# The second layer's expert products by high and low parts, with a ring of four experts' weights, in a two-layer graph and expert kernel

## The reference, cut to what matters

```python
def ffn_l1(x, Wg, bg, W1, b1, W2, b2):         # x: 1354 x 256, normed
    probs = softmax(x @ Wg + bg)
    comb = probs * top2_mask(x @ Wg + bg)
    out = zeros_like(x)
    for e in range(8):
        h = gelu(x @ W1[e] + b1[e])            # 256 -> 1024
        y = h @ W2[e] + b2[e]                  # 1024 -> 256
        out = out + comb[:, e:e+1] * y
    return x_residual + out
```

## Time and profile before

| what | value |
|---|---|
| median of 3 runs | 1015.61 us (1013.77 to 1016.34) |
| the profiled execution's own time | 1013.27 us |
| its span, first to last instruction | 1011.5 us |
| mean granted clock of TensorE | 0.896 |
| PE matmul busy | 828.7 us (82%) |
| VectorE / ScalarE / GpSimd busy | 519.4 / 383.4 / 104.4 us |
| bytes moved by DMA | 101.57 MB, mean 100 GB/s |

### The profile page before, as it was taken

The page is one execution under the profiler, slowest core; times in us unless marked ns, Lnnn a source line. Parts: engine busy times, 40 slices in busy tenths (PEclk is TensorE's granted clock), DMA queues, the critical chain, the costliest instruction groups (busy, mean ns, idle before and its releaser), DMA issues.

```text
span 1011.5 us, 12855 instructions
## 1 busy us (share of the span) xinstructions
PE 828.7 (82%) x3873; PEld 576.6 (57%) x3874; DVE 519.4 (51%) x1076; ACT 383.4 (38%) x787; POOL 104.4 (10%) x92
## 2 busy tenths in 40 slices
PE   5968799999999996229999266973549999999993
PEld 4856555555555435129999254862316666666663
DVE  4035587666666738529888236956412222222220
ACT  1004314655556564016666143312003444444441
POOL 2000000000000000260000400000621111111111
PEclk9987859999999998759999677997569999999997
DMA  7498811233230110042542482407231221221212
GB/s 262 166 265 310 214 32 38 58 72 78 70 78 23 33 28 9 10 150 106 198 164 83 138 336 86 143 20 313 77 109 28 32 32 32 32 33 32 35 27 65
DMA packets 53654, 101.57 MB, mean 100 GB/s; under 512 B 17614, under 2 KB 46054, under 8 KB 51920
## 3 DMA queue, kind: packets, MB, share of 16 engines
q1 hardware_dynamic: 47328, 92.20, 28.6%
q0 software_dynamic: 6288, 8.89, 4.8%
HBM read 70.80 MB, written 25.35 MB: 95 GB/s over the span
## 4 chain that ended last, share of the span: by engine, by line
PE 73%; DVE 10%; issue 5%; DMA 4%; POOL 3%; ACT 2%; SPq 1%; POOLq 0%; ACTq 0%; DVEq 0%
PE ps L1165 11%; PE ps L932 10%; PE ps L1147 10%; PE ps L912 6%; PE ps L863 5%; PE ps L924 5%; PE ps L1096 4%; PE ps L1017 4%; PE ps L1019 3%; PE ps L1018 3%; PE ps L1156 3%; DVE mx L1304 2%; PE ps L851 2%; PE ps L1111 1%; POOL xs_d L652 1%
## 5 line engine op out<-in xcount | busy, mean ns | idle before, releaser
L1304 DVE TENSOR_REDUCE mx<-ps 128x1 f32<-128x452 f32 x264 | 148.0, 620 | 68.6 <-PE ps L912 67.3
L718 ACT ACTIVATE expo<-ps 128x452 f32<-128x452 f32 x264 | 124.3, 552 | 110.7 <-PE ps L924 109.7
L932 PE MATMUL ps<-expo,v_st 128*64 128x452 f32 (+1 forms) x576 | 116.2, 525 | 0.0
L912 PE MATMUL ps<-k_st,q_st 96*128 96x452 f32 x264 | 111.3, 451 | 4.8 <-DMA k_st<-k_hi_d 4.6
L1165 PE MATMUL ps<-w_l,h 128*128 x464 | 109.3, 389 | 6.6 <-ACT h L834 4.1
L834 ACT ACT_TABLE_LOAD x29 | 37.2, 1283 | 191.1 <-PE ps L1156 191.1
L1147 PE MATMUL ps<-w_l,x1t_t 128*128 x232 | 107.6, 608 | 1.6 <-DVE x1t_t L1603 1.6
L1165 PEld LDWEIGHTS ps<-w_l,h 128*128 128x128 f32 x464 | 86.9, 192 | 24.7 <-issue 13.7
L924 PE MATMUL ps<-q_st,k_st 98*128 98x452 f32 x264 | 96.9, 388 | 2.5 <-ACT expo L718 2.0
L1615 DVE COPY h1pre<-ps 128x1024 f32<-128x1024 f32 x29 | 35.5, 1224 | 109.0 <-PE ps L1147 109.0
L912 PEld LDWEIGHTS ps<-k_st,q_st 96*128 96x128 f32 x264 | 54.4, 207 | 51.7 <-DVE mx L1304 30.8
(11 more groups left out here) (235 smaller groups left out, 1258.2 us busy)
## 6 DMA issues: line engine op xcount, KB each, us to landing
w_l<-w_l SPq DMA_DIRECT2D x8, 2053.0 KB, 8.3
w_l<-w_l SPq DMA_DIRECT2D x2, 8208.0 KB, 23.6
adj<-adj_t SPq DMA_DIRECT2D x22, 704.0 KB, 4.1
xs_d<-zeros SPq DMA_DIRECT2D x1, 3842.5 KB, 26.4
x1t<-xs_d SPq DMA_DIRECT2D x29, 132.5 KB, 2.1
q_st<-q_hi_d SPq DMA_DIRECT2D x16, 176.0 KB, 3.1
k_st<-k_hi_d SPq DMA_DIRECT2D x16, 176.0 KB, 4.1
xs_d<-zeros SPq DMA_DIRECT2D x1, 2176.0 KB, 10.2
```

The costliest lines, as they stand in the source:

```text
L718: act.activation(expo[g % 8][:, :], ps[:, 3 + g % 3, 0:QC], ACT.Exp, scale=SCALE).then_inc(s_exp, 1)
L912: pe.matmul(ps[:, i % 3, 0:KC], q_st[h % 3][0:3 * DK, (n // KB) * P:(n // KB + 1) * P], k_st[h % 3][0:3 * DK, (n % KB) * KC:(n % KB + 1) * ...
L932: return pe.matmul(ps[at:at + 2 * DK, 6 + g // T % 2, lo:hi], v_st[h % 2][:, kt, :], expo[g % 8][:, lo:hi], start=kt < 2, stop=kt == T - 1 ...
L1304: dve.tensor_reduce(mx4[:, n // KB, n % KB:n % KB + 1], ps[:, i % 3, 0:KC], AX_X, ALU.max).then_inc(s_mx, 1)
```

## The change

The second layer's products are now sums of three one-pass products of high and low parts, as in the first layer.

- **The split.** GpSimd, after L621, takes the weights of all eight experts in 32 parts of 128 x 1024: it loads a part, copies it rounded (`part_hi`), writes it to a scratch tensor in memory, subtracts, and writes the low part. The two part buffers lie where the router's buffers lie, so VectorE waits for all low writes ahead of `choose(0)`.
- **The ring.** Four experts' split weights lie on chip (4 x 8192 columns). SP loads slots 2 and 3 and slots 0 and 1 where it loaded the two halves before, and each of experts 4 to 7 into the slot of expert e - 4 once that one's tiles are done; PE waits for the loads that its tile needs.
- **The tile.** Rows and h1 are split into high and low parts by new operations on VectorE and ScalarE. In the down product the high and low weights of a block lie side by side, so one product of 512 columns makes both, and VectorE adds the two halves. PE's order becomes h1_turn(t + 1), xs1_in(t + 3), up1(t + 2), down1(t); the h1 parts have two buffers. Row loads move from SP's queue to GpSimd's. The biases get a buffer and a load of their own.

The diff, cut to its core:

```diff
+RING = 4
+SPLIT = 1024
+SLOTCOLS = 2 * B1AT
-        w_l1 = place("w_l1", [E, W1COLS])
+        w_ring = place("w_ring", [RING, SLOTCOLS], F32R)
+        part_hi = place("part_hi", [SPLIT], F32R)
+        cursor[0] = offsets["lgt"]
+        part = [place(f"part{i}", [SPLIT]) for i in range(2)]
+        cursor[0] = offsets["lgt"]
+        part_lo = [place(f"part_lo{i}", [SPLIT], F32R) for i in range(2)]
+        w_split_d = scratch("w_split_d", [P, E, SLOTCOLS])
+        PARTS1 = E * B1AT // SPLIT
...
         @block.sync
...
+            sp.wait_ge(s_hi_out, 16 * PARTS1)
+            for k in range(2):
+                sp.wait_ge(s_lo_out[k], 16 * (PARTS1 // 2))
+            sp.dma_start(w_ring.bitcast(F32)[:, RING // 2:RING, :], w_split_d[:, RING // 2:RING, :]).then_inc(s_w1, 16)
...
+            sp.dma_start(w_ring.bitcast(F32)[:, 0:RING // 2, :], w_split_d[:, 0:RING // 2, :]).then_inc(s_w1, 16)
-            sp.wait_ge(s_scat1, 2 * 16 * T)
-            sp.dma_start(x1t[:, :], xs1_d[0:P, :]).then_inc(s_x1l, 16)
...
+            for e in range(RING, E):
+                due = sp.value_load(ends_due[0:1, e - RING:e - RING + 1], min_val=PRIMED + 1, max_val=PRIMED + TILES1)
+                sp.wait_ge(s_y1_ps, due)
+                sp.dma_start(w_ring.bitcast(F32)[:, e - RING, :], w_split_d[:, e, :]).then_inc(s_ring, 16)
+                sp.wait_ge(s_ring, PRIMED + 16 * (e - RING + 1))
...
         @block.gpsimd
...
+            def load_part(n):
+                e, c = divmod(n, B1AT // SPLIT)
+                if n >= 2:
+                    pool.wait_ge(s_lo_out[n % 2], 16 * (n // 2))
+                pool.dma_start(part[n % 2][:, :], a["w_l1"][:, e, c * SPLIT:(c + 1) * SPLIT]).then_inc(s_part[n % 2], 16)
+
+            def split_rows(n, low):
+
+                e, c = divmod(n, B1AT // SPLIT)
+                if c < DT * F // SPLIT:
+                    return w_split_d[:, e, LO1 * low + c * SPLIT:LO1 * low + (c + 1) * SPLIT]
+                at = AT2 + 2 * (c * SPLIT - DT * F)
+                return w_split_d[:, e, at:at + 2 * SPLIT].rearrange("p (f b n) -> p f b n", b=2, n=D)[:, :, low, :]
...
+            load_part(0)
+            for n in range(PARTS1):
+                k = n % 2
+                if n + 1 < PARTS1:
+                    load_part(n + 1)
+                pool.wait_ge(s_part[k], 16 * (n // 2 + 1))
+                if n:
+                    pool.wait_ge(s_hi_out, 16 * n)
+                pool.tensor_copy(part_hi[:, :], part[k][:, :]).then_inc(s_part_split, 1)
+                pool.wait_ge(s_part_split, 2 * n + 1)
+                pool.dma_start(split_rows(n, 0), shaped(n, part_hi.bitcast(F32))).then_inc(s_hi_out, 16)
+                pool.tensor_tensor(part_lo[k][:, :], part[k][:, :], part_hi.bitcast(F32)[:, :],
+                                   ALU.subtract).then_inc(s_part_split, 1)
+                pool.wait_ge(s_part_split, 2 * n + 2)
+                pool.dma_start(split_rows(n, 1), shaped(n, part_lo[k].bitcast(F32))).then_inc(s_lo_out[k], 16)
+            pool.wait_ge(s_hi_out, 16 * PARTS1)
...
+            def load_rows1(t):
+                if t:
+                    pool.wait_ge(s_x1_ps, t)
+                    pool.wait_ge(s_share, t)
+                pool.dma_start(x1t[:, :], xs1_d[t * P:(t + 1) * P, :]).then_inc(s_x1l, 16)
+
+            pool.wait_ge(s_scat1, 2 * 16 * T)
+            for t in range(4):
+                load_rows1(t)
             pool.wait_ge(s_sum0, 16)
             for t in range(TILES1):
+                if t + 4 < TILES1:
+                    load_rows1(t + 4)
                 pool.wait_ge(s_y1, PRIMED + t + 1)
...
         @block.scalar
...
-                last.then_inc(s_h1, 1)
+                last.then_inc(s_h1f, 1)
+                act.wait_ge(s_h1f, t + 1)
+                if not first:
+                    act.wait_ge(s_y1_ps, PRIMED + t - 1)
+                act.activation(h1_hi[k][:, :, :], h1[:, :, :], ACT.Identity).then_inc(s_h1, 1)
...
         @block.tensor
...
+                slot_of = pe.value_load(tile_slot[0:1, bass.ds(t, 1)], min_val=0, max_val=RING - 1)
+                need = pe.value_load(tile_need[0:1, bass.ds(t, 1)], min_val=PRIMED, max_val=PRIMED + 16 * (E - RING))
+                pe.wait_ge(s_ring, need)
...
-                        mm = pe.matmul(ps[:, 2 + b, :], x1t_t[:, kt, :],
-                                       w_l1[:, bass.ds(e, 1), at:at + 512].rearrange("p a n -> p (a n)"),
-                                       start=kt == 0, stop=kt == DT - 1)
+                        pe.matmul(ps[:, 2 + b, :], x1_hi[:, kt, :], part_of(at), start=kt == 0, stop=False)
+                        pe.matmul(ps[:, 2 + b, :], x1_hi[:, kt, :], part_of(LO1 + at), start=False, stop=False)
+                        mm = pe.matmul(ps[:, 2 + b, :], x1_lo[:, kt, :], part_of(at), start=False, stop=kt == DT - 1)
...
+                    at = AT2 + f * 2 * D
+                    pe.matmul(ps[:, 6, :], h1_hi[k][:, f, :], part_of(at, 2 * D), start=f == 0, stop=False,
+                              skip_group_check=True)
+                    mm = pe.matmul(ps[:, 6, 0:D], h1_lo[k][:, f, :], part_of(at, D), start=False, stop=f == FT - 1,
+                                   skip_group_check=True)
...
         @block.vector
...
+            for k in range(2):
+                dve.wait_ge(s_lo_out[k], 16 * (PARTS1 // 2))
             choose(0)
...
+            def x1_split(t):
+                dve.wait_ge(s_x1_ps, t + 1)
+                dve.wait_ge(s_h1_ps, t)
+                turned_x = ps[:, 0, 0:DT * P].rearrange("p (c n) -> p c n", n=P)
+                dve.tensor_copy(x1_hi[:, :, :], turned_x).then_inc(s_x1hi, 1)
+                dve.wait_ge(s_x1hi, t + 1)
+                dve.tensor_tensor(x1_lo[:, :, :], turned_x, x1_hi.bitcast(F32)[:, :, :], ALU.subtract).then_inc(s_x1t, 1)
+
+            def h1_low(t, k):
+                dve.wait_ge(s_h1, t + 1)
+                dve.tensor_tensor(h1_lo[k][:, :, :], h1[:, :, :], h1_hi[k].bitcast(F32)[:, :, :],
+                                  ALU.subtract).then_inc(s_h1lo, 1)
...
+                dve.scalar_tensor_tensor(out=y1t[:, :], in0=ps[:, 6, D:2 * D], scalar=share[:, bass.ds(t, 1)], in1=y1t[:, :],
+                                         op0=ALU.mult, op1=ALU.add).then_inc(s_y1, 1)
...
+            def between(t, k, first=False):
+                x1_goal(t + 3)
+                h1_copy(t + 2)
+                x1_split(t + 3)
+                h1_low(t + 1, 1 - k)
+                y1_copy(t, first)
```

More of the change, by code:

```diff
@@ L48 @@
 W1COLS = B2AT
+RING = 4
+SPLIT = 1024
+SLOTCOLS = 2 * B1AT
+LO1 = DT * F
+AT2 = 2 * DT * F
 FAR = 1.0e6
@@ L234, in build_program @@
         ctx_odd = nat[:, :, :].rearrange("p t d -> p (t d)").rearrange("p (c n) -> p c n", c=DT)
-        cursor[0] = offsets["w_attn"]
+        cursor[0] = offsets["nt"]
+        h1pre = place("h1pre", [F])
+        h1 = place("h1", [FT, P])
+        x1_hi = place("x1_hi", [DT, P], F32R)
+        x1_lo = place("x1_lo", [DT, P], F32R)
+        y1t = place("y1t", [D])
+        assert cursor[0] <= offsets["const"]
+        cursor[0] = offsets["nat"]
+        h1_hi = [place("h1_hi0", [FT, P], F32R)]
+        h1_lo = [place("h1_lo0", [FT, P], F32R)]
         x1t = place("x1t", [ROW])
-        x1t_t = place("x1t_t", [DT, P])
-        y1t = place("y1t", [D])
         goal = place("goal", [TILES1], I32)
@@ L242, in build_program @@
         shares = place("shares", [E])
+        assert cursor[0] <= offsets["nt"]
+        cursor[0] = offsets["w_attn"]
+        h1_hi.append(place("h1_hi1", [FT, P], F32R))
+        h1_lo.append(place("h1_lo1", [FT, P], F32R))
         assert cursor[0] <= offsets["w_graph"]
-        cursor[0] = offsets["nt"]
-        h1pre = place("h1pre", [F])
-        h1 = place("h1", [FT, P])
-        assert cursor[0] <= offsets["const"]
         comb_t = lgt
@@ L1171, in _ @@
             up1(0)
+            xs1_in(1)
             h1_turn(0)
-            xs1_in(1)
-            with pe.Fori(0, TILES1 - 2) as t:
-                up1(t + 1)
-                xs1_in(t + 2)
-                down1(t)
-                h1_turn(t + 1)
-            up1(TILES1 - 1)
-            down1(TILES1 - 2)
-            h1_turn(TILES1 - 1)
-            down1(TILES1 - 1)
+            up1(1)
+            xs1_in(2)
+            with pe.Fori(0, (TILES1 - 3) // 2) as i:
+                for k in range(2):
+                    t = i * 2 + k
+                    h1_turn(t + 1)
+                    xs1_in(t + 3)
+                    up1(t + 2)
+                    down1(t, k)
+            t = TILES1 - 3
+            h1_turn(t + 1)
+            up1(t + 2)
+            down1(t, t % 2)
+            h1_turn(t + 2)
+            down1(t + 1, (t + 1) % 2)
+            down1(t + 2, t % 2)
         @block.vector
```

137 lines of the change are left out of this document (79 added, 58 removed).

## The result

The changed kernel takes **1031.26 us** (median of 4 runs, 1030.9 to 1035.89), the kernel before, measured beside it, 1015.93 (1013.77 to 1016.34): ratio 1.0165, 95% interval 1.0149 to 1.0181. It is slower by 15 us, as forecast and within 2 us of the forecast. The sum was right, its terms were not.

What follows compares the result with a forecast made beforehand. TensorE was taken to bound attention and the second layer's expert tiles. 1013.3 - 37 (tiles) + 10 (ring) + 39 (split) + 2 (attention) = 1027, about 1030 as a median; range 978 to 1085, the forecast's own 1018 to 1060.

Steps and rivals of the forecast that it cites:

- choose(0) 28 to 70 us late: The forecast's own case: the routing waits for the split's last low write; 1018 to 1060 us in all, chance 0.38.
- rival 1's partial case: The split ahead of choose(0) is partly hidden, late by 10 to 25 us, total 1000 to 1012; chance 0.09.
- Products and the tile's period: Second layer's tiles: one-pass products cut the period by 1.41 to 6.93 us; 41 less 4 at the edges, 37 gained.
- Both stay under 6.93 and both are out of PE's way: In a tile, ScalarE's 5.7 us and VectorE's 5.1 us fit within the 6.93 us period without delaying PE.
- the thin cover of the two single buffers: In tiles, y1t's addition has a margin of 1.3 us and the row load about 1; said to hold.
- The ring: Four reloads of 4096 KB beside the tiles delay row loads and additions: 2.5 us each, 10 lost, bounds 0 and 40.
- Rival 3: Single buffers y1t and x1t set the tiles' pace during reloads, or h1_low holds GpSimd's issues: gain 10 or 20, chance 0.06.
- The split: GpSimd's 32-part chain ahead of choose(0): 9.47 and 11.41 us a part against 9.21 available, ending at 450, 39 us late.
- The break-even of 10.05 a part: Mean time per split part at which the kernel would equal the one before; the forecast's mean was 10.44.
- the prediction's estimate from it: From the skill page's 3.2 us for 512 KB: 8.9 us a split part, 284 in all, split hidden; stands behind the first rival.
- Attention beside the split: Split transfers join attention's small ones on SP's queue, where stage waits are few: 2 us lost.
- in attention VectorE has no such work: VectorE's 262 attention operations are nearly all maxima from PSUM, so GpSimd's subtraction costs 0; were it wrong, some 32 x 2.

Runs made afterwards that it cites:

- three part buffers: The changed kernel with a third buffer for GpSimd's split parts, so that no load waits for the low write two parts back: 1033.13 us, ratio 1.0179.

## Why the prediction was right, and where

The time was right within 2 us because two terms were wrong by much the same amount with opposite signs: the reloads cost 23 us more than forecast, the split and attention beside it 28 less. That is luck. The forecast asked for choose(0) 28 to 70 us late; it was 13 to 16 late, which is rival 1's partial case (10 to 25), priced at 0.09. Only the ring's cost brought the time back into the forecast's range. By the prediction's own steps:

- **Products and the tile's period** (37 gained): mechanism right, size nearly. Without reloads the tiles gave 259.3 - 225.5 = 33.8. Product times held within 0.01 us. "Both stay under 6.93 and both are out of PE's way" held for ScalarE and VectorE; the thin cover of the two single buffers, of which the prediction said that it holds, gave 0.24 a tile away, as the runs with two of each show (6.92).
- **The ring** (10 lost; bounds 0 and 40): this is the step that failed. "I take 2.5 each, near the lower end since these transfers are small." Measured, 33 for four, 8 each. Being small didn't help: beside a reload the load of rows and the addition landed in 10 to 11.5 us instead of 3.5 and 3.9. The rows gave the upper bound, 40, from margins of 1 to 1.3 us and engines held for 11.8, and the estimate should have stayed near it. Rival 3 named the place (the single buffers during reloads) but priced it at 1.2 us a tile.
- **The split** (39 late): the chain and what is queued behind it were right, the sizes of two terms were not. The issue of a direct transfer is 0.54, or 0.84 with the gap ahead of a write, not the indirect one's 1.27 with its gap, and the runs of 1 KB add 0.23 and not 0.97; the other way, the subtraction took 2.39 (2.23), the copy 1.05 (0.90), and from the low write's issue to the next load it was some 4.2 on the mean (0.57 to 0.79 of issue, 3.5 of waiting) where 3.8 was put. Pace 9.53 instead of 10.44; the choice's own wait for the last write was 5.8 us and not 39. The break-even of 10.05 a part leaves out the 2 us put on attention; with them it is 9.99. The page weighed there, DMA: Bandwidth & Descriptors of the Trainium skill, says that many descriptors come before their cost shows, and the trace agrees in the main: 384 more runs added 0.23 us to an issue. Its 3.2 us for 512 KB was too little beside other traffic, where the medians were 3.5 to 4.5, and the split that the prediction's estimate from it would have hidden (284 us in all) wasn't hidden.
- **Attention beside the split** (2 lost): "in attention VectorE has no such work" was wrong. The maxima go unhindered (0.62 each, before and after), but the shift made from them is held (2.81 us at the most instead of 0.17), and the last normalization multiplies and adds with both inputs on chip, on the path to the logits. From the last maxima to the end of the last product it took 55.9 us instead of 49.2, 6.7 more; with the heads' 1.4 that is 8, of which 7.6 were left at the logits (302.5 us after the clearing instead of 294.9), and not 2. With the wait of 5.8 this makes the 13.4. The rule cited from the page SBUF — State Buffer (Who interferes with whom) of the Trainium skill, two inputs in SBUF contend and a reduce doesn't, agrees with 2.83 against 0.63 and with the maxima beside the heads. It was cited rightly and applied to too short a list of operations; and as the prediction took it, for two inputs alone, it leaves out the shift and the copies, which read one input and were held as well.
- Sum as it should have been, from the profiled execution: 1013.3 - 34 + 33 + 13 + 3 (execution to execution ahead of the split) + 2 (between choice and tiles) = 1030.

The sign hung on the reloads: without them, or with paced ones and two buffers, the same split leaves a faster kernel (999.3, 992.5). Whether it hung on the split too is not shown. The kernel without it was 0.6% slower than before (1020.4), but its reloads cost 8.5 us more than the changed kernel's; less that, it would be at about 1012, level with before within the 3 us that the prediction allows.

## What to carry to other kernels

A big transfer beside a loop whose small transfers have single buffers costs most of its own duration each time (here 8 us for each transfer of 12.9); give those buffers a second copy and hand the big one out in pieces that wait for each other, small enough not to hold the small ones, large enough not to be late. Before putting work on GpSimd beside a stage, list VectorE's operations on that stage's critical path with their operands, the short ones and those at its edges too, not only those with the most counts. And a helper's wait can be what protects the stage beside it: making the helper faster made its neighbour slower.

## What was not expected of the hardware

- GpSimd's issue of a direct transfer: 0.54 us for 128 runs, 0.77 for 512. One that overlapped an addition's issue took 1.14.
- VectorE is held until GpSimd's operation ends even where its own has one input on chip: a copy of 128 x 272 took 2.83 instead of 0.29, one of 128 x 352 2.73 instead of 0.34, one of 128 x 11 2.81 instead of 0.17. These three began 0.2 to 0.4 us before the subtraction, while GpSimd issued a transfer, and ended at most 0.2 after it. The products of 128 x 452 issued 0.02 us behind GpSimd's subtraction of 2.35 took 2.83: the rest of that operation and half a microsecond. Beside a clearing, which reads nothing, such a product wasn't held, and an operation of one input was.
- Runs of 32 KB or of 4 KB in the big transfer made 8 us of 33; the bytes in flight made some 18 more, by the estimate above.
- 276 GB/s beside the heads (three part buffers) against 220 (two) raised the heads' own loads from 5.0 to 7.6 us.
